# Incidence product of a graph network as one fp32r matmul of 258 columns, with a new order of the degree and edge steps

## The chip, the cores and the metric

One core of a Trainium2 chip runs the whole program. The metric is the time on the device in microseconds, from start to end of one execution. The kernel before took 1463.44 us in the median of three runs (1463.33 to 1463.59).

## The reference, cut to what matters

128 graphs with 128 nodes of 256 features go through four layers. Each layer's output is added to its input and normalised over the features. The first layer is a hypergraph convolution, used twice with one and the same operator; this change concerns its making:

```python
H  = (adj != 0).astype(x.dtype)                # incidence, 128 x 128
w  = adj.reshape(N, -1)[:, :C]                 # first row of adj
Dn = 1.0 / einsum('nce,ne->nc', H, w)          # where the sum is > 0
Be = 1.0 / H.sum(axis=1)                       # one value per hyperedge
G  = Dn * H @ (Be * H^T)                       # the operator of both convolutions
h  = layer_norm(relu(G (x W1^T) + b1), gamma, beta)
y  = G (h W2^T) + b2 + x
x  = _layernorm(x + y)
```

The second layer is a mean over the neighbours with two weights, the third has three graph convolutions, the fourth one graph convolution with a mask. Each is followed by the sum and `_layernorm`. The G line is the kernel's way of grouping, not a line of the reference.

## The kernel before, in words

The graphs are worked on in 64 pairs. The kernel is a software pipeline written out by hand: a table LAG says how many iterations after its start a pair reaches each stage, so that iteration n works on pair n in the stage G, on pair n-1 in R and P, on n-2 in xT, XAB and AXB, on n-3 in Ax2, H1, H1W and H2, on n-4 in H2W, AP3, Ax3 and TK, and on n-5 in the last normalisation F. Iterations 0 to 2 are written out in a function fill on each engine, iterations 3 to 68 run through a function body. Each engine has its own list of operations in a fixed order, and semaphores join them. Nothing is reordered: an operation that waits holds all that stands behind it on its engine.

TensorE (PE) works in the order R, G, xT, H2W, Ax2, XAB, H1, AP3, P, Tr, AXB, H1W, Ax3, Gx, GP, H2, TK (lines 499 to 533). Most products split both factors into a high part rounded to fp32r and a low part, the rest, and add three fp32r products (line 256). G, Tr, Gx, GP, xT, Ax2, Ax3 and H2 are plain fp32 instead.

The stages around the change, for pair q = n+1 (edges) and pair n (degrees):

- DVE makes the incidence HT (line 888), counts it (892), takes the maximum with 1 (897) and the reciprocal be_inv (904).
- POOL multiplies HT with be_inv into BH (1207). ACT copies the first row of the adjacency into BH's last column (weight_column, 645).
- In the next iteration PE forms G, per graph one fp32 product of HT with the 129 columns of BH into one bank (288). Column 128 of the result is the degree.
- DVE takes maximum (866), reciprocal (870) and the inverse degree dinv (874), and scales G's PSUM result into Gd (881). PE transposes Gd (303), ACT copies it out as GT (611).

In the body of the iteration DVE alternates degree and edge steps (lines 1085 to 1100). After them it makes the third normalisation's sum (1108), which waits for AP3, statistics, the split of XAB (858), the third's inverse and shift (828, 832), the variance of the hidden layer (921, 924), the reciprocal h_rstd (930), the operand p_f of GP (940), the aggregate (959), the second sum (969) and the first sum (976). ACT applies the third normalisation (560), takes the mean's square (623) and the root h_std (627). POOL's order is n_s (1246), the low parts r_lo (1188), two sums of squares (1194, 1196), A_lo, the fourth sum (1254), h_lo, BH (1207), x2c (1265), xb (1215), and h_lo of the second hidden layer.

## Time and profile before

| | |
|---|---|
| median of three runs | 1463.44 us |
| the profiled execution's own time | 1463.48 us |
| its span, first to last instruction | 1461.7 us |
| mean granted TensorE clock | 0.991 of full speed |
| busy: DVE, ACT, POOL | 1080.4, 1056.8, 851.7 us |
| data moved by DMA | 47.04 MB, mean 32 GB/s |

In the profile PE is TensorE's matmuls, PEld its weight loads, DVE VectorE, ACT ScalarE, POOL GpSimd. A matmul's end is modelled and overlaps the next one's start, so the distance between starts tells what one costs. An fp32 matmul appears as two records. A row of a timeline gives the start in us from the span's start, the duration of the row, the engine, the line, the operation, the tiles (output <- inputs), the shape and the number of instructions merged into the row; behind it stands the idle time of the engine before it, with what ended it. Line 254 is the helper that issues every matmul, line 541 ACT's copy, line 810 the statistics.

### The profile page before, as it was taken

Reading aid. Unit: us, or ns where it says so; the run is one execution under the profiler, and the core shown is the slowest. Engines: PE = TensorE matmul, PEld = TensorE weight load, DVE = VectorE, ACT = ScalarE, POOL = GpSimd, SP = SyncE. Lnnn points to the kernel's source line nnn. Section 1 sums busy time; section 2 is a strip of 40 time slices with the busy share of each in tenths; the row PEclk is TensorE's granted clock in tenths of the full one; section 3 lists DMA queues with packets and bytes.
Section 4 is the critical chain, followed back from the end, with each engine's and each line's share of the span. In section 5 each row is a group of like instructions: output and inputs, shape, how many; then the busy total and the mean of one; then the engine's idle time right before and its main releaser. Section 6 shows DMA issues by size and latency. Waiting matters only on the chain. (4 is left out here: it accounts for less than half of the span.)

```text
span 1461.7 us, 33281 instructions
## 1 busy us (share of the span) xinstructions
PE 1416.2 (97%) x10896; PEld 1353.8 (93%) x10896; DVE 1080.4 (74%) x3744; ACT 1056.8 (72%) x2442; POOL 851.7 (58%) x776
## 2 busy tenths in 40 slices
PE   7899999999999999999999999999999999999974
PEld 6799999999999999999999999999999999999973
DVE  6667777777777777777777777777777777777663
ACT  4577777778777777777777777777777777777863
POOL 4565565565566566566566566566566566566542
PEclk9999999999999999999999999999999999999997
DMA  4001101101101101101101101101100100110000
GB/s 135 23 12 37 38 19 37 38 19 37 37 20 37 38 19 37 38 19 37 38 20 37 38 19 37 38 24 32 38 26 30 38 28 29 37 30 16 15 16 22
DMA packets 29946, 47.04 MB, mean 32 GB/s; under 512 B 3408, under 2 KB 12240, under 8 KB 29776
## 3 DMA queue, kind: packets, MB, share of 16 engines
q1 hardware_dynamic: 29776, 44.91, 9.8%
q8 instruction: 89, 1.46, 0.4%
q14 instruction: 81, 0.66, 0.2%
HBM read 28.12 MB, written 16.78 MB: 31 GB/s over the span
## 5 line engine op out<-in xcount | busy, mean ns | idle before, releaser
L1180 POOL TENSOR_TENSOR h_lo<-h_f,h_hi 128x512 fp32r<-128x512 f32 x128 | 166.2, 1298 | 373.4 <-ACT h_hi L541 373.4
L560 ACT ACTIVATE x<-n_s,n_shift,n_rstd 128x256 f32<-128x256 f32 x384 | 208.4, 590 | 101.0 <-DVE n_shift L832 101.0
L810 DVE BATCH_NORM_STATS2 n_st<-n_s 128x6 f32<-128x256 f32 x512 | 188.1, 409 | 7.6 <-POOL n_s L1254 5.2
L555 ACT ACTIVATE n_std<-n_mv,eps_c 128x2 f32<-128x2 f32 x256 | 74.7, 292 | 158.3 <-DVE n_mv L815 158.2
L1188 POOL TENSOR_TENSOR r_lo<-r_f,r_hi 128x512 fp32r<-128x512 f32 x128 | 163.5, 1299 | 36.6 <-ACT r_hi L541 36.4
L1246 POOL TENSOR_TENSOR n_s<-tk,mask 128x512 f32<-128x512 f32 x64 | 66.7, 1042 | 165.7 <-issue 150.4
L254 PE MATMUL psum<-v_hi,h_hi 128*128 128x256 f32 x512 | 148.9, 291 | 5.0 <-issue 5.0
L254 PE MATMUL psum<-A_f,x 128*128 128x128 f32 x1024 | 142.1, 282 | 5.4 <-ACT x L560 4.8
L254 PE MATMUL psum<-w2c_hi,r_hi 128*128 128x258 f32 x512 | 145.9, 285 | 0.5 <-POOL r_lo L1188 0.5
L254 PE MATMUL psum<-w2c_hi,r_lo 128*128 128x258 f32 x512 | 146.0, 285 | 0.0
L254 PE MATMUL psum<-w2c_lo,r_hi 128*128 128x258 f32 x512 | 144.8, 283 | 0.0
L254 PE MATMUL psum<-v_hi,h_lo 128*128 128x256 f32 x512 | 144.1, 282 | 0.0
L254 PE MATMUL psum<-v_lo,h_hi 128*128 128x256 f32 x512 | 144.0, 281 | 0.0
L254 PE MATMUL psum<-gx_hi,w1T_hi 128*128 128x256 f32 x512 | 143.9, 281 | 0.0
L254 PE MATMUL psum<-gx_hi,w1T_lo 128*128 128x256 f32 x512 | 143.3, 280 | 0.0
L254 PE MATMUL psum<-gx_lo,w1T_hi 128*128 128x256 f32 x512 | 143.3, 280 | 0.0
L565 ACT ACTIVATE h_f<-psum,columns 128x256 f32<-128x256 f32 x256 | 107.7, 473 | 48.9 <-PE psum L254 48.9
L254 PEld LDWEIGHTS psum<-A_f,x 128*128 128x128 f32 x1024 | 126.0, 193 | 8.1 <-ACT x L560 5.4
L1108 DVE TENSOR_TENSOR n_s<-psum,x2c 128x512 f32<-128x512 f32 x64 | 44.3, 692 | 87.0 <-PE psum L254 87.0
L254 PE MATMUL psum<-wab_hi,x1T_hi 128*128 128x512 f32 x256 | 106.8, 417 | 0.0
L802 DVE TENSOR_TENSOR ax_lo<-psum,ax_hi 128x512 fp32r<-128x512 f32 x128 | 87.8, 686 | 25.3 <-ACT ax_hi L541 25.3
L565 ACT ACTIVATE r_f<-psum,columns 128x256 f32<-128x256 f32 x256 | 99.1, 463 | 3.9 <-PE psum L254 3.9
(141 smaller groups left out, 5044.1 us busy)
## 6 DMA issues: line engine op xcount, KB each, us to landing
x_in<-x_in_dram SPq DMA_DIRECT2D x64, 256.0 KB, 3.0
out<-x SPq DMA_DIRECT2D x64, 256.0 KB, 2.0
at_in<-adjT SPq DMA_DIRECT2D x64, 128.0 KB, 2.3
x<-v_in SPq DMA_DIRECT2D x3, 256.0 KB, 5.8
n_s<-w2T_in SPq DMA_DIRECT2D x2, 256.0 KB, 3.7
r_f<-w1T_in SPq DMA_DIRECT2D x2, 256.0 KB, 4.7
h_f<-wab_in SPq DMA_DIRECT2D x2, 256.0 KB, 6.0
rows<-rows_in SPq DMA_DIRECT2D x1, 256.0 KB, 6.1
```

The source lines that it names most:

```text
L254: return pe.matmul(o, a, b, start=start, stop=stop)
L555: act.activation(nm.std[:], nm.mv[:, :, 1], ACT.Sqrt, bias=eps_c[:, 0:1]).then_inc(nm.rooted, 1)
L560: last = act.activation(dst[:, g, :], nm.s[:, g, :], ACT.Identity, scale=nm.rstd[:, g:g + 1], bias=nm.shift[:, g:g + 1])
L565: return act.activation(dst[:, m].rearrange("p g c -> p (g c)"), psum[:, BANK[stage] + extra, (m % 2) * 2 * C:(m % 2 + 1) * 2 * C], ACT.Re ...
L802: return dve.tensor_tensor(dst[1][:], src, f(dst[0][:]), ALU.subtract).then_inc(signal, 1)
L810: last = dve.bn_stats(nm.st[:, g, :], nm.s[:, g, :])
L1108: dve.tensor_tensor(n3.s[:].rearrange("p g d -> p (g d)"), flat(BANK["AP3"]), x2c[(k - 4) % 2][:].rearrange("p g d -> p (g d)"), ALU.add). ...
L1180: return pool.tensor_tensor(dst[1][:], src, f(dst[0][:]), ALU.subtract).then_inc(signal, 1)
L1188: pool.tensor_tensor(r_s[1][:, half], r_f[:, half], f(r_s[0][:, half]), ALU.subtract).then_inc(r_lo[h], 1)
L1246: pool.tensor_tensor(n4.s[:], tk[:], bc(mask[:], [C, 2, D], 2), ALU.mult).then_inc(tk_masked, 1)
```

## The change

BH becomes 258 columns wide and fp32r: 128 columns of HT times the rounded be_inv (be_r), 128 of HT times the rest (be_rest), one with the rounded weight and one with its rest. HT is fp32r; it holds zeros and ones. One fp32r matmul per graph multiplies HT with all 258 columns, each graph into a bank of its own (5 and 7; for pair 2 6 and 7). ACT's weight_column becomes round_edges, which also rounds be_inv and stands behind out_XAB instead of ahead of it. POOL makes the two rests and two products. DVE first adds the two degree columns, then takes maximum, reciprocal and dinv from SBUF, scales the second half into Gl and adds the scaled first half, graph by graph. In the body the degree chain stands whole ahead of the four edge steps. ACT takes the hidden layer's mean square ahead of applying the third normalisation and h_std right behind it. DVE makes p and the aggregate ahead of the fourth normalisation's inverse and shift, and the second sum ahead of the split of Ax3. POOL's x2c waits for hve. Some banks and waits of the filling stage move.

```diff
-        HT = sb("HT", [2, C])
+        HT = sb("HT", [2, C], F32R)
-        BH = sb("BH", [2, C + 1])
+        BH = sb("BH", [2, 2 * C + 2], F32R)
...
             def G(n, k):
                 p = n
                 pe.wait_ge(bh_made, upto(p))
-                pe.wait_ge(w_made, upto(p))
+                pe.wait_ge(w_lo, upto(p))
+                if begun(p - 2) and not first(n, 2):
+                    pe.wait_ge(p_made, upto(p - 2))
                 if begun(p - 5):
                     pe.wait_ge(ax3_lo, upto(p - 5))
                 for g in range(2):
-                    last = mm(psum[:, BANK["G"], g * (C + 1):(g + 1) * (C + 1)], HT[:, g, :], BH[:, g, :],
-                              True, True)
+                    last = mm(psum[:, bank("G", p)[g], 0:2 * C + 2], HT[:, g, :], BH[:, g, :], True, True)
...
             def P(n, k):
...
+                if not first(n, 2):
+                    pe.wait_ge(gd_made, upto(n))
...
-            def weight_column(n, k):
+            def round_edges(n, k):
                 q = n + 1
                 act.wait_ge(at_loaded[(k + 1) % RING], at_count(q, k + 1))
                 if begun(n):
                     act.wait_ge(pe_did["G"], upto(n))
-                copy(BH[:, :, C:C + 1], at_in[:, (k + 1) % RING, :, 0:1]).then_inc(w_made, 1)
+                copy(BH[:, :, 2 * C:2 * C + 1], at_in[:, (k + 1) % RING, :, 0:1]).then_inc(w_hi, 1)
+                act.wait_ge(be_made, upto(q))
+                if begun(q - 1):
+                    act.wait_ge(bh_made, upto(q - 1))
+                copy(be_r[:], be_inv[:]).then_inc(be_hi, 1)
...
-                if active("prep", n):
-                    weight_column(n, k)
                 if active("XAB", n):
                     out_XAB(n, k)
+                if active("prep", n):
+                    round_edges(n, k)
...
                     root(n3, p)
+                if active("P", n):
+                    square_mean(n, k)
+                if active("AP3", n):
+                    p = n - 4
...
                     apply(n3, p, x3)
+                if active("P", n):
+                    root_h(n, k)
+                if active("Tr", n):
+                    copy_GT(n, k)
                 if active("F", n):
                     root(n4, n - 5)
-                if active("P", n):
-                    square_mean(n, k)
-                if active("Tr", n):
-                    copy_GT(n, k)
-                if active("P", n):
-                    root_h(n, k)
...
             def degree_max(n, k):
                 dve.wait_ge(pe_did["G"], upto(n))
-                dve.tensor_scalar(dn_max[:], dn, TINY, None, ALU.max).then_inc(dn_1, 1)
+                dve.tensor_reduce(dn[:], out_G(n, 2 * C, 2 * C + 2), AX_X, ALU.add).then_inc(dn_0, 1)
+                dve.wait_ge(dn_0, upto(n))
+                dve.tensor_scalar(dn_max[:], dn[:], TINY, None, ALU.max).then_inc(dn_1, 1)
...
-                dve.tensor_tensor(Gd[:], g_dn[:, :, 0:C], bc(dinv[:], [C, 2, C], 2), ALU.mult).then_inc(gd_made, 1)
+                dve.tensor_tensor(Gl[:], out_G(n, C, 2 * C), bc(dinv[:], [C, 2, C], 2), ALU.mult).then_inc(gl_made, 1)
+                dve.wait_ge(gl_made, upto(n))
+                for g in range(2):
+                    last = dve.scalar_tensor_tensor(out=Gd[:, g, :], in0=psum[:, bank("G", n)[g], 0:C],
+                                                    scalar=dinv[:, g:g + 1], in1=Gl[:, g, :],
+                                                    op0=ALU.mult, op1=ALU.add)
+                last.then_inc(gd_made, 1)
...
                 if active("G", n):
-                    degree_max(n, k)
+                    scale_G(n, k)
                 if active("prep", n):
-                    edges(n, k)
-                if active("G", n):
-                    degree_recip(n, k)
-                if active("prep", n):
-                    edge_count(n, k)
-                if active("G", n):
-                    degree_inverse(n, k)
-                if active("prep", n):
-                    edge_max(n, k)
-                if active("G", n):
-                    make_Gd(n, k)
-                if active("prep", n):
-                    edge_inverse(n, k)
+                    prep(n, k)
...
                 if active("AXB", n):
                     node_degree_max(n, k)
+                if active("AXB", n):
+                    node_degree_recip(n, k)
+                if active("P", n):
+                    wide_invert(n, k)
+                    make_p(n, k)
+                if active("AXB", n):
+                    make_agg(n, k)
                 if active("F", n):
                     invert(n4, n - 5)
-                if active("P", n):
-                    wide_invert(n, k)
+                    shift(n4, n - 5)
                 if active("AXB", n):
-                    node_degree_recip(n, k)
-                if active("F", n):
-                    shift(n4, n - 5)
-                if active("P", n):
-                    make_p(n, k)
-
-                if active("AXB", n):
-                    make_agg(n, k)
+                    sum_n2(n, k)
                 if active("Ax3", n):
                     dve.wait_ge(ax3_hi, upto(n - 4))
                     split_lo(ax3, flat(BANK["Ax3"]), ax3_lo)
-                if active("AXB", n):
-                    sum_n2(n, k)
...
             def make_BH(n, k):
                 q = n + 1
-                pool.wait_ge(be_made, upto(q))
+                pool.wait_ge(w_hi, upto(q))
+                pool.tensor_tensor(BH[:, :, 2 * C + 1:2 * C + 2], at_in[:, (k + 1) % RING, :, 0:1],
+                                   f(BH[:, :, 2 * C:2 * C + 1]), ALU.subtract).then_inc(w_lo, 1)
+                pool.wait_ge(be_hi, upto(q))
+                pool.tensor_tensor(be_rest[:], be_inv[:], f(be_r[:]), ALU.subtract).then_inc(be_lo, 1)
                 if begun(n):
                     pool.wait_ge(pe_did["G"], upto(n))
-                pool.tensor_tensor(BH[:, :, 0:C], HT[:], bc(be_inv[:], [C, 2, C], 2), ALU.mult).then_inc(bh_made, 1)
+                pool.tensor_tensor(BH[:, :, 0:C], f(HT[:]), bc(f(be_r[:]), [C, 2, C], 2), ALU.mult)
+                pool.wait_ge(be_lo, upto(q))
+                pool.tensor_tensor(BH[:, :, C:2 * C], f(HT[:]), bc(be_rest[:], [C, 2, C], 2),
+                                   ALU.mult).then_inc(bh_made, 1)
...
                     pool.wait_ge(n2.done, upto(p))
+                    if active("P", n):
+                        pool.wait_ge(hve, upto(n - 1))
```

## Rows read from the trace of the kernel before

**Rows 1.** The page, part 1: busy time, share of the span and instructions.
```profile
PE 1416.2 (97%) x10896; PEld 1353.8 (93%) x10896; DVE 1080.4 (74%) x3744; ACT 1056.8 (72%) x2442; POOL 851.7 (58%) x776
```
**Rows 2.** Timeline of PE in one iteration in the middle.
```profile
814.98 0.61 PE L254 MATMUL psum<-BH,HT 128*128 128x129 f32 x4
815.43 0.65 PE L368 MATMUL psum<-ident,x 128*128 128x128 f32 x4
...
822.45 0.28 PE L254 MATMUL psum<-h2w_hi,A_hi 128*128 128x256 f32 x1
...
823.16 0.28 PE L254 MATMUL psum<-w2c_hi,r_hi 128*128 128x258 f32 x1
...
828.81 1.14 PE L254 MATMUL psum<-A_f,x 128*128 128x128 f32 x8
829.79 1.06 PE L254 MATMUL psum<-GT,x_in 128*128 128x128 f32 x8
```
**Rows 3.** Timeline of ACT, same iteration.
```profile
814.03 0.29 ACT L555 ACTIVATE n_std<-n_mv,eps_c 128x2 f32<-128x2 f32 x1 [0.20 <-DVE n_mv L815]
...
818.64 0.62 ACT L541 ACTIVATE ax_hi<-psum 128x512 fp32r<-128x512 f32 x1
...
822.65 0.84 ACT L565 ACTIVATE h_f<-psum,columns 128x256 f32<-128x256 f32 x2 [0.34 <-PE psum L254]
...
827.65 1.09 ACT L560 ACTIVATE x<-n_s,n_shift,n_rstd 128x256 f32<-128x256 f32 x2 [1.60 <-DVE n_shift L832]
...
829.40 0.20 ACT L627 ACTIVATE h_std<-h_veps 128x2 f32<-128x2 f32 x1
...
835.85 0.29 ACT L555 ACTIVATE n_std<-n_mv,eps_c 128x2 f32<-128x2 f32 x1 [0.20 <-DVE n_mv L815]
```
**Rows 4.** Timeline of DVE, same iteration.
```profile
819.90 0.15 DVE L866 TENSOR_SCALAR dn_max<-psum 128x2 f32<-128x2 f32 x1
...
821.63 0.41 DVE L881 TENSOR_TENSOR Gd<-psum,dinv 128x256 f32<-128x256 f32 x1
...
823.36 0.69 DVE L1108 TENSOR_TENSOR n_s<-psum,x2c 128x512 f32<-128x512 f32 x1 [1.25 <-PE psum L254]
...
826.56 0.97 DVE L832 SCALAR_TENSOR_TENSOR n_shift<-n_mv,n_rstd 128x2 f32<-128x2 f32 x1
...
829.84 0.88 DVE L940 SCALAR_TENSOR_TENSOR p_f<-psum,h_rstd,betaW 128x256 f32<-128x256 f32 x2
...
832.01 0.68 DVE L969 SCALAR_TENSOR_TENSOR n_s<-agg,x 128x512 f32<-128x512 f32 x1
...
833.22 0.67 DVE L976 SCALAR_TENSOR_TENSOR n_s<-xb,psum 128x512 f32<-128x512 f32 x1
```
**Rows 5.** Groups of DVE by line and shape, 600 to 1000 us: busy, mean ns.
```profile
L897 DVE TENSOR_SCALAR be<-ht_count 128x2 f32<-128x2 f32 x19 | 13.1, 688 | 0.0
...
L892 DVE TENSOR_REDUCE ht_count<-HT 128x2 f32<-128x256 f32 x19 | 8.0, 421 | 0.0
```
**Rows 6.** Timeline of DVE in the filling stage, POOL idle.
```profile
3.70 0.17 DVE L897 TENSOR_SCALAR be<-ht_count 128x2 f32<-128x2 f32 x1
```
**Rows 7.** Timeline of POOL, the iteration of rows 2 to 4.
```profile
817.84 2.54 POOL L1188 TENSOR_TENSOR r_lo<-r_f,r_hi 128x512 fp32r<-128x512 f32 x2 [0.42 <-ACT r_hi L541]
820.34 1.35 POOL L1194 TENSOR_TENSOR sq<-sq 128x512 f32<-128x512 f32 x1
...
822.46 0.74 POOL L1180 TENSOR_TENSOR A_lo<-at_in,A_hi 128x256 fp32r<-128x256 f32 x1
823.15 1.30 POOL L1254 TENSOR_TENSOR n_s<-n_s,x 128x512 f32<-128x512 f32 x1
824.40 1.30 POOL L1180 TENSOR_TENSOR h_lo<-h_f,h_hi 128x512 fp32r<-128x512 f32 x1
825.64 0.63 POOL L1207 TENSOR_TENSOR BH<-HT,be_inv 128x256 f32<-128x256 f32 x1
...
827.46 1.30 POOL L1215 TENSOR_TENSOR xb<-x_in,b2half 128x512 f32<-128x512 f32 x1
```

More of the change, by code:

```diff
@@ L25 @@
 BANK = dict(R=0, Ax2=0, Tr=0, GP=0, H1=1, Gx=1, XAB=2, AXB=2, TK=2, H2=3, xT=4, P=4,
-            H2W=6, H1W=6, G=7, AP3=7, Ax3=7)
+            H2W=6, H1W=6, G=(5, 7), AP3=7, Ax3=7)
 BANKS = 8
@@ L67, in build @@
         at_in = sb("at_in", [RING, 2, C])
-        HT = sb("HT", [2, C])
-        ht_count, be, be_inv = sb("ht_count", [2]), sb("be", [2]), sb("be_inv", [2])
-        BH = sb("BH", [2, C + 1])
-        dn_max, dn_inv, dinv = sb("dn_max", [2]), sb("dn_inv", [2]), sb("dinv", [2])
-        Gd = sb("Gd", [2, C])
+        HT = sb("HT", [2, C], F32R)
+        ht_count, be = sb("ht_count", [2]), sb("be", [2])
+        be_inv, be_r, be_rest = sb("be_inv", [2]), sb("be_r", [2], F32R), sb("be_rest", [2])
+        BH = sb("BH", [2, 2 * C + 2], F32R)
+        dn, dn_max, dn_inv, dinv = sb("dn", [2]), sb("dn_max", [2]), sb("dn_inv", [2]), sb("dinv", [2])
+        Gl, Gd = sb("Gl", [2, C]), sb("Gd", [2, C])
         GT = [sb(f"GT{b}", [2, C]) for b in range(2)]
@@ L132, in build @@
         pe_R0 = sem("pe_R0")
-        ht_made, ht_counted, be_max, be_made, bh_made = (
-            sem(s) for s in ("ht_made", "ht_counted", "be_max", "be_made", "bh_made"))
-        dn_1, dn_2, dn_3, gd_made = sem("dn_1"), sem("dn_2"), sem("dn_3"), sem("gd_made")
-        w_made, gt_made, gx_hi, gx_lo = (sem(s) for s in ("w_made", "gt_made", "gx_hi", "gx_lo"))
+        ht_made, ht_counted, be_max, be_made, be_hi, be_lo, bh_made = (
+            sem(s) for s in ("ht_made", "ht_counted", "be_max", "be_made", "be_hi", "be_lo", "bh_made"))
+        dn_0, dn_1, dn_2, dn_3, gl_made, gd_made = (sem(s) for s in ("dn_0", "dn_1", "dn_2", "dn_3", "gl_made", "gd_made"))
+        w_hi, w_lo, gt_made, gx_hi, gx_lo = (sem(s) for s in ("w_hi", "w_lo", "gt_made", "gx_hi", "gx_lo"))
         r_relu, r_hi = [sem(f"r_relu{j}") for j in range(2)], [sem(f"r_hi{j}") for j in range(2)]
@@ L170, in bank @@
         def bank(stage, pair):
+            if stage == "G" and pair == 2:
+                return 6, 7
             if stage == "Tr" and pair in (1, 2):
-                return 3
+                return 3 * pair
             if stage == "GP" and pair == 0:
@@ L296, in Tr @@
                     pe.wait_ge(eye_loaded, 16)
-                if first(n, 2):
-                    pe.wait_ge(betaW_made, 1)
                 pe.wait_ge(gd_made, upto(p))
@@ L363, in xT @@
                 pe.wait_ge(n1.done, upto(p))
-                if not first(n, 2):
+                if first(n, 2):
+                    pe.wait_ge(betaW_made, 1)
+                else:
                     pe.wait_ge(p_made, upto(p))
@@ L655, in fill @@
                 act.wait_ge(table_loaded, 1)
-                weight_column(-1, -1)
+                round_edges(-1, -1)
                 act.wait_ge(columns_loaded, 16)
@@ L661, in fill @@
                 split_w1(1)
-                weight_column(0, 0)
+                round_edges(0, 0)
                 relu_r(1, 1, 0)
@@ L677, in fill @@
                 root_h(1, 1)
+                round_edges(1, 1)
                 relu_r(2, 2, 0)
@@ L695, in fill @@
                 out_XAB(2, 2)
+                round_edges(2, 2)
                 for dst, src in ((v_s[2], v_f[2]), (wk_s, wk_f)):
@@ L859, in split_xbw, with out_G @@
                                   f(xbw[0][:, :, 0:D]), ALU.subtract).then_inc(xbw_lo, 1)
-            g_dn = psum[:, BANK["G"], 0:2 * (C + 1)].rearrange("p (g c) -> p g c", g=2)
-            dn = g_dn[:, :, C]
+            def out_G(n, lo, hi):
+                b = bank("G", n)
+                return psum[:, b[0]:b[1] + 1:b[1] - b[0], lo:hi]
             def degree_max(n, k):
                 dve.wait_ge(pe_did["G"], upto(n))
-                dve.tensor_scalar(dn_max[:], dn, TINY, None, ALU.max).then_inc(dn_1, 1)
+                dve.tensor_reduce(dn[:], out_G(n, 2 * C, 2 * C + 2), AX_X, ALU.add).then_inc(dn_0, 1)
+                dve.wait_ge(dn_0, upto(n))
+                dve.tensor_scalar(dn_max[:], dn[:], TINY, None, ALU.max).then_inc(dn_1, 1)
             def degree_recip(n, k):
@@ L873, in degree_inverse @@
                 dve.wait_ge(dn_2, upto(n))
-                dve.scalar_tensor_tensor(out=dinv[:], in0=dn, scalar=0.0, in1=dn_inv[:],
+                dve.scalar_tensor_tensor(out=dinv[:], in0=dn[:], scalar=0.0, in1=dn_inv[:],
                                          op0=ALU.is_gt, op1=ALU.mult).then_inc(dn_3, 1)
@@ L1009, in fill @@
                 split_gx(0, 0)
+                prep(0, 0)
                 split_w1(1)
@@ L1148, in body @@
                     make_agg(n, k)
+                if active("F", n):
+                    invert(n4, n - 5)
+                    shift(n4, n - 5)
+                if active("AXB", n):
+                    sum_n2(n, k)
                 if active("Ax3", n):
```

12 lines of the change are left out of this document (3 added, 9 removed).

## The prediction

> **What bounds the kernel now.** I read the page first, then the timeline of each engine over one iteration in the middle (pair p enters at iteration n = p), because the average says little here: PE is busy for 97% of the span [rows 1]. In the PE timeline the reader is to see that stages follow each other without a hole, and also that the modelled busy time hides small waits: eight passes of 128 columns run in 0.98 us at the Ax3 stage (828.81 to 829.79), although a pass of that width takes 0.11 us (G's four passes fill 814.98 to 815.43), which makes 0.89 [rows 2]. So the Ax3 stage waits 0.09 us, for the third normalisation.
>
> In the DVE and ACT timelines I look for a chain that closes on itself. ACT's root of the first normalisation starts at 814.03 and the next at 835.85, 21.82 us later [rows 3]. From the first, ACT works on without a gap to the copy ax_hi at 818.64; DVE takes over (ax_lo, degree chain, third sum at 823.36), ACT normalises (827.65) and takes the root h_std (829.40), DVE makes p (829.84), the sums at 832.01 and 833.22, and the statistics that release 835.85 [rows 3, 4]. In this chain DVE waits for PE only once, for the third sum at 823.36, after Gd was done at 822.04 (821.63 + 0.41). The kernel is therefore held by two things of nearly one length: PE's work, and this chain through DVE and ACT. A saving on PE is worth its price only if the chain shortens too.
>
> A third view, DVE's groups, shows what the chain is sensitive to. The two-element maximum be takes 0.69 us in the loop and 0.17 us in the filling stage when POOL is idle [rows 5, 6]. In the loop it ends when POOL's sum of squares ends (820.34 + 1.35 = 821.69). In the same way the shift at 826.56 takes 0.97 us and ends at 827.53, where POOL's x2c hands over to xb (827.46) [rows 4, 7]. DVE operations that read and write SBUF alone can thus be held until the running POOL operation ends; Gd, which reads PSUM, starts beside POOL at 821.63 and takes its 0.41 us.
>
> **PE's part.** Removed: four passes of G, 0.45 us. Added: two fp32r matmuls of 258 columns. The row nearest to them is the third product, six fp32r matmuls of 256 columns in 0.71 us (822.45 to 823.16), 0.118 us each [rows 2]; I take 0.12, so 0.24 us. PE saves 0.21 us in each iteration. Bounds: 0.17 (a switch of format costing 0.02 a matmul) to 0.23. The Trainium skill, "TensorE: Matmul & The Clock Gate", section "Back-to-back issue gap", gives N/2.4 + 2.5 ns, an estimate of 0.110 us for 258 columns; by it PE would save 0.23 us. The trace's 0.118 decides. The waits of PE on p_made (for the bank) and of P on gd_made cost nothing: p is a whole iteration old at G, and the third product ahead of P waits for gd_made already.
>
> **The degree chain (DVE).** I walk the new order in the clock of this iteration, with ax_hi at 818.64 as fixed point, since ACT's run from 814.03 to there is unchanged. A dependent two-element step costs 0.17 [rows 6] and some 0.03 to hand over.
> - The reduction of the two degree columns reads PSUM and takes the place of dn_max: 819.90 to 820.06.
> - dn_max now reads SBUF. It asks at 820.10; POOL's r_lo runs until 820.38 (817.84 + 2.54) [rows 7]. Done 820.41. The reciprocal ends at 820.61.
> - dinv now reads two SBUF tiles, as the held shift does. It asks at 820.65, and POOL's sum of squares has been running since 820.34. Done about 821.74.
> - Gl, like Gd before, 0.41: 821.78 to 822.19. Two halves of 128 columns, by the 0.41 of Gd less half its columns at about one nanosecond each, 0.30 each: Gd is done at 822.8, against 822.04 before. The third product is due at 822.45, so PE waits 0.4 us there.
> Bounds for Gd: 821.7 if neither step is held, 823.0. I take 822.8, because both held forms have a row.
>
> **The edges behind it.** HT asks at 822.74 while POOL makes A_lo (until 823.20): done 823.35. The count takes 0.42 [rows 5], to 823.8. The maximum be then asks while POOL makes the fourth sum (from about 823.2, 1.30 long) and is held until 824.5, as it was held before until 821.69. be_inv is done at 824.7, and the third sum starts at 824.65 instead of 823.36: 1.3 us late [rows 4, 7].
>
> **ACT.** round_edges waits for be_made at 824.7. Queued behind it are the relus h_f (822.65 before) and their rounding. The two-element copy takes about 0.20, like h_std; h_f starts at 824.85, and 0.84 + 0.62 (the length of ax_hi) later h_hi is done at 826.4 [rows 3]. POOL's h_lo moves from 824.40 to 826.4 and ends at 827.7, 2.0 us later; its user on PE, H1W, is itself pushed back by the 0.4 of the third product and stands behind the whole of P, so I take nothing for it and keep 0.2 as the upper bound.
>
> **POOL.** After h_lo come two small subtractions and two products instead of one. The small ones have no row: POOL's 256 elements take 0.74 and 512 take 1.30 [rows 7], which leaves 0.18 of fixed cost; bounds 0.1 and 0.3. The products take 0.63 each. So BH is ready at about 829.2, x2c (behind its new wait for hve, which is earlier) runs until 830.45, and xb until 831.7, against 828.76 before. For the next G this is hidden, there being some 7 us to it; for the lock it is not.
>
> **Third normalisation and what follows.** From third sum to shift is 3.20 us (823.36 to 826.56): it asks at 827.85, between POOL operations, and is done at 828.0 instead of 827.53. This is where the old hold of 0.83 goes. The normalisation takes 1.09 from 828.1, h_std 0.20 behind it, so p starts at 829.55, 0.3 us earlier than 829.84: placing the mean square ahead and the DVE reciprocals in time takes the old detour away. p and agg take 1.57 together (832.01 less 0.60 for ax_lo less 829.84), to 831.12. Now the inverse and the shift of the fourth normalisation stand here: the shift asks at 831.3 and is held by xb until 831.73. The second sum starts at 831.77, ax_lo 0.60 later, gx_lo, and the first sum at 833.57 instead of 833.22. **The chain is 0.35 us longer**, 22.17 instead of 21.82.
>
> **Sum.** 59 iterations hold all stages (n = 5 to 63): 59 x 0.35 = 20.7 us. The filling stage gets ACT's copy, POOL's subtraction and second product, and the longer scaling ahead of the first graph products: 0.2 + 0.2 + 0.6 + 0.8, less what the shorter G gives; I take 2 us, bounds 0 and 5. The profiled execution took 1463.48 us (span 1461.7), as good as the median of 1463.44. Forecast 1463.5 + 20.7 + 2 = 1486.
>
> The Trainium skill speaks against the change at just this point: "SBUF — State Buffer", section "SBUF: two separate sides", says that a DVE operation with two SBUF inputs or in a 2-port mode and a GpSimd operation exclude each other for a whole instruction. The trace agrees for be and the shift; by that rule the new dn_max and dinv join them.
>
> **The rivals.**
> - *The chain keeps its length.* If xb is done by 831.3 (small POOL operations shorter, h_lo earlier), the shift of the fourth is free and the first sum starts at 833.15: nothing gained, nothing lost in the loop. 1463.5 + 2 = 1465.5, and with a few hundredths either way 1461 to 1470. For it: only 0.4 us separates the two. Against it: between h_lo and xb POOL has no idle time in which to catch up.
> - *Faster, PE decides.* If the two-element steps are not held, or be slips in between two POOL operations, the third sum starts as soon as PE delivers it. Then the 0.21 of G and the 0.09 ahead of Ax3 count, and as much again ahead of the product with p, which the earlier p removes: 59 x 0.4 = 24 us, 1442 with the filling stage. With only dinv held, PE's 0.4 us wait before the third product takes that back and 59 x 0.08 = 5 us less 2, about 1461, is left. The point from which it decides is a third sum before about 824.1. For it: p_f, agg and the sums would all have slack. Against it: be is held in the mean of 19 rows.
> - *Slower still.* The shift of the third meets the first product of POOL (0.63) instead of a gap: 0.3 to 0.5 us more an iteration, 1504 to 1515.
> - *The product isn't faster.* If fp32r with 258 columns ran in two passes, PE would keep its 0.45 us; with the chain as the bound the forecast would stand.
>
> **How the numbers follow.** The chain longer with xb in the way 0.48; the chain unchanged 0.20; PE decides, wholly or in part, 0.25; slower still 0.07. About 0.2% (3 us) is what a measurement of this kernel can tell from no change. Of the unchanged case I give 0.12 to within 3 us, 0.06 to slower and 0.02 to faster, and 0.01 of the PE case lies within too; so faster 0.26, same 0.13, slower 0.61. The range runs from 1450, which leaves out the full PE case (0.12), to 1498, which leaves out the last (0.07). The forecast case's own range is 1474 to 1498.
>
> **What would show it.** BH,HT as two matmuls 0.12 apart; dinv at about 1.1 us instead of 0.15; be still at 0.5 to 0.7; the third sum no longer waiting for PE; ACT's h_f waiting for be_inv; n_shift short at the third and long at the fourth; PE with idle time ahead of the transposes of x1 and the third product. A third sum that still waits for PE would prove me wrong, whatever the total.

## The result, and the profile after

The changed kernel takes 1473.88 us (median of 4 runs, 1473.70 to 1474.56) against 1463.51 us beside it: a ratio of 1.007, 95% interval 1.0052 to 1.0087. That is slower by 10.4 us, a little less than half of the 22.5 us forecast. Spans of the profiled executions: 1471.9 us after, 1461.7 us before.

The page, part 1 (answers to [rows 1]):
```profile
PE 1408.7 (96%) x10768; PEld 1350.3 (92%) x10768; DVE 1213.3 (82%) x3936; ACT 1061.1 (72%) x2506; POOL 907.9 (62%) x968
```
DVE is busy for 133 us more. dinv alone is about 55 of them (0.15 us before, 1.01 now, 64 times): two elements for each row, which wait for POOL. "Held" below means this, a DVE operation whose row is long because a POOL operation is running.

The times below are of one iteration in which ax_hi starts at 825.76. It started at 818.64 in the iteration of [rows 3], so **take off 7.12 us to compare a time with the forecast or with rows of before**.

Timeline of PE (answers to [rows 2]):
```profile
822.45 0.41 PE L257 MATMUL psum<-BH,HT 128*128 128x258 f32 x2
822.69 0.60 PE L374 MATMUL psum<-ident,x 128*128 128x128 f32 x4
...
829.52 0.28 PE L257 MATMUL psum<-ax_hi,v_lo 128*128 128x256 f32 x1
830.03 0.36 PE L257 MATMUL psum<-h2w_hi,A_hi 128*128 128x256 f32 x1 [0.23 <-DVE Gd L898]
...
836.43 1.08 PE L257 MATMUL psum<-A_f,x 128*128 128x128 f32 x8
837.35 1.06 PE L257 MATMUL psum<-GT,x_in 128*128 128x128 f32 x8
```
G fills 0.24 us (822.45 to 822.69) instead of 0.45. The third product now waits for Gd: at 0.12 us for a matmul it would start at 829.64, and it starts 0.39 us later. The distance from Ax3 to Gx is 0.92 us, against 0.98.

Timeline of ACT (answers to [rows 3]):
```profile
821.15 0.29 ACT L560 ACTIVATE n_std<-n_mv,eps_c 128x2 f32<-128x2 f32 x1 [0.20 <-DVE n_mv L826]
...
825.76 0.62 ACT L546 ACTIVATE ax_hi<-psum 128x512 fp32r<-128x512 f32 x1
...
831.82 0.20 ACT L546 ACTIVATE be_r<-be_inv 128x2 fp32r<-128x2 f32 x1 [2.22 <-DVE be_inv L924]
831.93 0.82 ACT L570 ACTIVATE h_f<-psum,columns 128x256 f32<-128x256 f32 x2
...
835.20 1.10 ACT L565 ACTIVATE x<-n_s,n_shift,n_rstd 128x256 f32<-128x256 f32 x2 [0.73 <-DVE n_shift L843]
836.20 0.19 ACT L632 ACTIVATE h_std<-h_veps 128x2 f32<-128x2 f32 x1
...
843.06 0.30 ACT L560 ACTIVATE n_std<-n_mv,eps_c 128x2 f32<-128x2 f32 x1 [0.20 <-DVE n_mv L826]
```
One root of the first normalisation follows the other after 21.91 us, against 21.82 in [rows 3]. Over all full iterations the means are 21.917 and 21.841 us (distance of PE's stage R from one pair to the next). This distance is called the period below.

Timeline of DVE (answers to [rows 4]):
```profile
827.21 0.33 DVE L880 TENSOR_SCALAR dn_max<-dn 128x2 f32<-128x2 f32 x1
...
827.77 1.01 DVE L888 SCALAR_TENSOR_TENSOR dinv<-dn,dn_inv 128x2 f32<-128x2 f32 x1
828.82 0.42 DVE L895 TENSOR_TENSOR Gl<-psum,dinv 128x256 f32<-128x256 f32 x1
829.27 0.61 DVE L898 SCALAR_TENSOR_TENSOR Gd<-psum,dinv,Gl 128x128 f32<-128x128 f32 x2
829.80 0.61 DVE L908 TENSOR_SCALAR HT<-at_in 128x256 fp32r<-128x256 f32 x1
...
830.90 0.69 DVE L917 TENSOR_SCALAR be<-ht_count 128x2 f32<-128x2 f32 x1
831.62 0.17 DVE L924 RECIPROCAL be_inv<-be 128x2 f32<-128x2 f32 x1
831.73 0.69 DVE L1116 TENSOR_TENSOR n_s<-psum,x2c 128x512 f32<-128x512 f32 x1
...
834.93 0.16 DVE L843 SCALAR_TENSOR_TENSOR n_shift<-n_mv,n_rstd 128x2 f32<-128x2 f32 x1
...
835.19 0.47 DVE L944 SCALAR_TENSOR_TENSOR h_veps<-h_var,eps_c 128x2 f32<-128x2 f32 x1
...
836.62 0.88 DVE L960 SCALAR_TENSOR_TENSOR p_f<-psum,h_rstd,betaW 128x256 f32<-128x256 f32 x2
837.42 0.87 DVE L979 SCALAR_TENSOR_TENSOR agg<-psum,rdeg,xa 128x256 f32<-128x256 f32 x2
...
838.39 0.31 DVE L843 SCALAR_TENSOR_TENSOR n_shift<-n_mv,n_rstd 128x2 f32<-128x2 f32 x1
838.62 0.68 DVE L989 SCALAR_TENSOR_TENSOR n_s<-agg,x 128x512 f32<-128x512 f32 x1
...
840.42 0.68 DVE L996 SCALAR_TENSOR_TENSOR n_s<-xb,psum 128x512 f32<-128x512 f32 x1
```
dinv takes 1.01 us. The third sum follows be_inv without a gap and no longer waits for PE.

Timeline of POOL (answers to [rows 7]):
```profile
827.47 1.29 POOL L1199 TENSOR_TENSOR sq<-sq 128x512 f32<-128x512 f32 x1
828.84 0.73 POOL L1201 TENSOR_TENSOR sq<-sq 128x256 f32<-128x256 f32 x1
...
830.21 1.35 POOL L1266 TENSOR_TENSOR n_s<-n_s,x 128x512 f32<-128x512 f32 x1
833.49 1.28 POOL L1185 TENSOR_TENSOR h_lo<-h_f,h_hi 128x512 fp32r<-128x512 f32 x1 [1.93 <-ACT h_hi L546]
834.73 0.20 POOL L1210 TENSOR_TENSOR BH<-at_in,BH 128x2 fp32r<-128x2 f32 x1
...
835.03 0.61 POOL L1216 TENSOR_TENSOR BH<-HT,be_r 128x256 fp32r<-128x256 f32 x1
835.60 0.61 POOL L1218 TENSOR_TENSOR BH<-HT,be_rest 128x256 fp32r<-128x256 f32 x1
836.17 1.28 POOL L1279 TENSOR_TENSOR x2c<-x,rows 128x512 f32<-128x512 f32 x1
837.41 1.27 POOL L1227 TENSOR_TENSOR xb<-x_in,b2half 128x512 f32<-128x512 f32 x1
```
dinv ends at 828.78, with the sum of squares (827.47 + 1.29 = 828.76). be ends at 831.59, with the fourth sum (831.56). The second sum starts at 838.62, as xb ends (838.68).

**Where the 10.4 us are.** Three marks in each trace divide the difference of the two spans, 10.2 us: G of pair 5 (the end of the filling stage), the period, and the rest.

| | before | after | difference |
|---|---|---|---|
| G of pair 5 starts | 94.53 | 99.14 | +4.6 |
| 59 periods | 59 x 21.841 | 59 x 21.917 | +4.5 |
| the rest, to the end of the span | 78.6 | 79.7 | +1.1 |

### The profile page after: what moved, and what is told of

It reads as the page before. It is cut to its first block and busy times, and to the rows that moved or that the text cites. A ratio compares the mean times of both kernels' runs of the same rounds, so it can differ in the third digit from the quotient of the medians.

```text
span 1471.9 us, 33596 instructions
## 1 busy us (share of the span) xinstructions
PE 1408.7 (96%) x10768; PEld 1350.3 (92%) x10768; DVE 1213.3 (82%) x3936; ACT 1061.1 (72%) x2506; POOL 907.9 (62%) x968
## 5 line engine op out<-in xcount | busy, mean ns | idle before, releaser
L546 ACT ACTIVATE be_r<-be_inv 128x2 fp32r<-128x2 f32 x64 | 13.0, 203 | 133.6 <-DVE be_inv L924 133.6
L257 PEld LDWEIGHTS psum<-v_hi,h_hi 128*128 128x128 f32 x512 | 97.3, 190 | 5.5 <-issue 5.5
```

Of the source, the lines that this page charges most:

```text
L257: return pe.matmul(o, a, b, start=start, stop=stop)
L546: return act.activation(o, i, ACT.Copy)
```

## The experiments

Each ran beside the kernel before (medians 1463.2 to 1464.4 us). The period is the mean over some 55 iterations.

### Degree sums in PSUM

```diff
+        dn = psum[:, 7, 510:512]
-        dn, dn_max, dn_inv, dinv = sb("dn", [2]), ...
+        dn_max, dn_inv, dinv = ...
```


> The changed kernel, but the sum of the two degree columns is left in PSUM, so that the maximum and dinv read PSUM. Theory 1 (the chain through DVE, ACT and POOL is the bound, and dinv is held by POOL's sum of squares): dinv 0.15 us instead of 1.01, Gd 1.1 to 1.2 us earlier, the third sum waits for PE again, period 21.4 us instead of 21.91, so 1474 - 59 x 0.5 = 1444 us. Rival A (PE's own work grew: it reads the wider fp32r operand, its first stage R takes 2.86 instead of 2.82 us): the period stays within 0.1 us of 21.9, 1468 to 1474. Rival B (ACT's wait for be_made is what costs, not the degrees): be_made comes only about 0.6 to 1 us earlier and ACT still waits; the gain is about half, 1455 to 1465.

Measured: 1436.78 us, ratio 0.9807 (0.9789 to 0.9826), period 21.322. That is theory 1, with 37 us instead of its 30; both rivals are out. Timeline of DVE:
```profile
806.37 0.16 DVE L881 TENSOR_SCALAR dn_max<-psum 128x2 f32<-128x2 f32 x1
...
806.76 0.16 DVE L889 SCALAR_TENSOR_TENSOR dinv<-psum,dn_inv 128x2 f32<-128x2 f32 x1
...
807.94 0.28 DVE L909 TENSOR_SCALAR HT<-at_in 128x256 fp32r<-128x256 f32 x1
...
808.72 0.17 DVE L918 TENSOR_SCALAR be<-ht_count 128x2 f32<-128x2 f32 x1
...
809.63 0.69 DVE L1117 TENSOR_TENSOR n_s<-psum,x2c 128x512 f32<-128x512 f32 x1 [0.54 <-PE psum L258]
```
and of POOL:
```profile
806.61 1.31 POOL L1200 TENSOR_TENSOR sq<-sq 128x512 f32<-128x512 f32 x1
808.00 0.82 POOL L1202 TENSOR_TENSOR sq<-sq 128x256 f32<-128x256 f32 x1
```
dinv runs in the middle of the sum of squares. be, now earlier, comes 0.1 us before POOL's short sum ends (808.82) and is hardly held. The third sum waits for PE again. So 37.1 us of the changed kernel's time (1473.9 less 1436.8) are this one placement of two numbers per row.

### All the new orders on the old product

```diff
@@ body of before, DVE, ACT and POOL @@
+   the degree chain whole, ahead of the four edge steps
+   ACT: square_mean ahead of apply(n3), root_h and copy_GT behind it
+   DVE: wide_invert, make_p, make_agg ahead of invert(n4), shift(n4)
+   POOL: wait_ge(hve, ...) ahead of x2c
```


> The kernel before with all the new orders (degrees ahead of edges, mean square ahead of the third normalisation, DVE's tail, x2c behind hve), but the old fp32 product with 129 columns and one product on POOL. Theory 1: no degree step reads SBUF beside POOL's sum of squares, so nothing there is held; the third shift is free, the waits of PE ahead of Ax3 and of the product with p go; period 21.84 - 0.28 = 21.56, 1447 us. Rival A: the orders are worth nothing by themselves, 1463. A third possibility, that x2c pushed back delays xb and with it the fourth shift: 1455 to 1463.

Measured: 1446.32 us, ratio 0.9873 (0.9856 to 0.9891), period 21.560, as theory 1 said. The orders alone gain 17 to 18 us; the wide product on top of them costs 27.6 us (1473.9 less 1446.3).

### The wide product in the old orders

```diff
@@ body of after @@
-   all four lines above
```


> The wide fp32r product with all that it needs, but degrees and edges alternating as before, ACT's and DVE's old orders, x2c without its wait. Theory 1: dn_max is held by r_lo, HT by the sum of squares, be by A_lo, all ahead of Gd in the alternating order; Gd comes about 1.5 us later than in the changed kernel, PE waits some 1.9 us ahead of the third product, period about 23.3 us, 1550 us. Rival A (PE's own work): as the changed kernel or less, 1463 to 1475. Rival B (ACT's wait): about as the changed kernel, 1470 to 1480.

Measured: 1501.92 us, ratio 1.0256 (1.0235 to 1.0276), period 22.378. The direction holds; the size is less than half of what was expected (38 us over the kernel before instead of 87). Timeline of DVE:
```profile
806.95 0.81 DVE L942 SCALAR_TENSOR_TENSOR h_veps<-h_var,eps_c 128x2 f32<-128x2 f32 x1
...
820.56 0.28 DVE L906 TENSOR_SCALAR HT<-at_in 128x256 fp32r<-128x256 f32 x1
...
821.21 0.80 DVE L886 SCALAR_TENSOR_TENSOR dinv<-dn,dn_inv 128x2 f32<-128x2 f32 x1
821.93 0.16 DVE L915 TENSOR_SCALAR be<-ht_count 128x2 f32<-128x2 f32 x1
```
h_veps is held by xb (in POOL's timeline 806.46, 1.28 long). dinv is held until 822.01, and be, asked right behind it, is not held at all although POOL has its next sum to do. That sum starts at 822.07: it waits for the sum before it, and the two stand 0.08 us apart in every version here, so be passes in a pause of POOL's own.

### Degrees and edges alternating again, the rest as changed

```diff
-                    scale_G(n, k)
-                    prep(n, k)
+                    degree_max(n, k)
+                    edges(n, k)
+                    degree_recip(n, k)
...
```


> The changed kernel with degrees and edges alternating as before, all else new. Theory 1: as for the product alone, Gd 1.5 us later, 1540 to 1550 us. Rival B (ACT's wait for be_made): be_made comes at about the same time as in the changed kernel, so 1470 to 1478.

Measured: 1478.71 us, ratio 1.0098 (1.0076 to 1.0121), period 21.971. A miss of theory 1: I expected each two-element step to meet a POOL operation of its own. In the trace dn_max is released at POOL's boundary and HT, queued right behind it, goes through unheld in 0.28 us. Of the two-element steps of degrees and edges dn_max keeps its 0.33, only dinv is held for long (0.80 us), and be takes 0.15. Two chains interleaved share a boundary. Rival B's number was nearly met (1470 to 1478), but not for its reason: be_inv comes earlier than in the changed kernel, and the third sum waits for PE again. A hold has moved elsewhere as well, to the shift of the second normalisation, which meets POOL's h_lo (it takes 0.15 us in the changed kernel). Timeline of DVE:
```profile
811.77 0.69 DVE L1128 TENSOR_TENSOR n_s<-psum,x2c 128x512 f32<-128x512 f32 x1 [1.06 <-PE psum L257]
...
822.93 0.89 DVE L843 SCALAR_TENSOR_TENSOR n_shift<-n_mv,n_rstd 128x2 f32<-128x2 f32 x1
```
That hold isn't what sets the period, since the version with the sums in PSUM has it too (0.89 us) at 21.32. Gd does: it ends 4.25 us after ax_hi's start instead of 4.12, the third product starts 0.15 us behind it in both, and 0.13 us more than the 21.84 of the version without the maximum (below) is 21.97.

### The wide product in the old orders, sums in PSUM

The edits of the wide product in the old orders and of the PSUM version together.

> The wide product with the orders of the kernel before, and the two degree sums kept in PSUM. Theory (two separate costs: SBUF-only two-element steps held behind POOL, and an order in which the mean square stands behind the third normalisation): only the hold of dinv goes (0.80 us in the wide product with the old orders), h_veps stays held by POOL's xb (0.81 us there), so the period falls from 22.38 by 0.1 to 0.3 us, to 22.1 to 22.3, 1484 to 1496 us. Rival (the degree chain alone was the price of the wide product): the period falls to that of the kernel before less what G saves, 21.6 to 21.7, 1450 to 1456 us.

Measured: 1489.19 us, ratio 1.0179 (1.0162 to 1.0196), period 22.207, in the middle of the theory's range. dinv takes 0.15, h_veps still 0.82, be 0.69. The PSUM sums are worth 12.7 us in the old orders and 37.1 in the new ones.

### The maximum with 1 left out

```diff
-                dve.tensor_scalar(be[:], ht_count[:], 1.0, None, ALU.max)...
-                dve.reciprocal(be_inv[:], be[:]).then_inc(be_made, 1)
+                dve.reciprocal(be_inv[:], ht_count[:]).then_inc(be_made, 1)
```


> The changed kernel without the maximum of the edge count with 1 (left out; every edge here has members, and the inverse is taken of the count itself). The held two-element step is gone, so be_inv and the third sum can come 0.5 to 0.7 us earlier. Theory (one chain through the third sum sets 21.92, but a second loop through Gd, the third product, R, the relus and ax_hi stands 0.07 us behind it at about 21.84): the period falls only to 21.84 to 21.86, 1469 to 1471 us, with the wait of the third product for Gd unchanged at about 0.4 us. Rival A (one chain only): the period falls by 0.5 us or so to 21.4, 1440 to 1447 us. Rival B (be's hold passes on to be_inv, which now meets the same POOL operation): unchanged, 1473 to 1475 us.

Measured: 1467.98 us, ratio 1.0029 (1.0012 to 1.0045), period 21.839. The gain stops at the second loop, as the theory said (21.84), and the third product still waits 0.41 us for Gd. A saving of 0.7 us on the chain gave 0.078.

### The fourth normalisation's steps back ahead of p

```diff
                     node_degree_max(n, k)
+                    invert(n4, n - 5)
                     wide_invert(n, k)
                     node_degree_recip(n, k)
+                    shift(n4, n - 5)
                     make_p(n, k)
...
```


> The changed kernel with DVE's operations behind the third normalisation in the order of the kernel before (inverse and shift of the fourth ahead of p and of the node degree's inverse, ax3_lo ahead of the second sum). Theory of the second loop: the shift of the fourth, asked earlier, falls between or into POOL's products and p is late by what it is held; if it isn't held the first chain shortens by up to 0.17 us and the loop through Gd caps the gain at 21.84, 1469 us. Rival: the order of the tail is worth what the forecast's last steps say, the shift held 0.3 to 0.5 us ahead of p, which is on the chain: period 22.2 to 22.4, 1490 to 1502 us.

Measured: 1493.49 us, ratio 1.0206 (1.0190 to 1.0221), period 22.259. p starts 1.18 us after h_std instead of 0.42 (836.62 less 836.20). DVE waits there for ACT's root of the fourth, and the shift is held 0.38 us. The rival of the expectation was right.

### ACT's old order in the changed kernel

```diff
                     root(n3, p)
-                    square_mean(n, k)
                     apply(n3, p, x3)
-                    root_h(n, k)
-                    copy_GT(n, k)
                     root(n4, n - 5)
+                    square_mean(n, k)
+                    copy_GT(n, k)
+                    root_h(n, k)
...
-                        pool.wait_ge(hve, upto(n - 1))
```


> The changed kernel with ACT's order of before (mean square, copy of GT and root of h behind the application of the third normalisation and the root of the fourth), without POOL's wait for hve. Theory (the order is worth about as much here as on the old product, 0.2 to 0.5 us an iteration, since h_veps is then asked behind the hand-over to xb and is held by it): period 22.2 to 22.4, 1490 to 1502 us. Rival (after the third sum's own lateness of 1.2 us the mean square has slack): period 21.92 to 21.98, 1474 to 1478 us.

Measured: 1543.73 us, ratio 1.0549 (1.0532 to 1.0565), period 23.090. The theory's direction, three times its size. Where DVE waits in the middle of the kernel (for what, us in total, times, longest):
```profile
DVE h_var L939 <- ACT h_mean L628: 78.9, 53, 1.8
```
ACT comes to the mean only behind the application of the third normalisation, which is itself late, and the root of the fourth. DVE idles 1.5 us for it in each iteration (78.9 by 53), and h_veps behind it is held for 0.70. Beside a degree chain that stands in front, the move of the mean square is worth 1.17 us an iteration; beside alternating chains it was 0.41, with p's move (22.378 less 21.971).

### Each order alone on the old product

```diff
@@ body of before: square order only @@
+   ACT, DVE (p, agg) and POOL lines of the new orders
@@ body of before: degree order only @@
+   the degree chain whole, ahead of the four edge steps
```


> The kernel before with two of the change's orders: ACT's mean square, root of h and copy of GT ahead of the third normalisation's application and of the fourth's root, and DVE's p and agg ahead of the fourth's inverse and shift (with POOL's wait for hve). Old product, degrees and edges still alternating. Theory (the whole gain of 17 to 18 us that all orders together give on the old product comes from here, since in before the third sum waits for PE and Gd is in time anyhow): period 21.55 to 21.60, 1446 to 1449 us. Rival (the two reorderings need each other): less than half of it, 1455 to 1463 us.

> The kernel before with the degree chain ahead of the edges on DVE and nothing else. Theory (Gd comes about 1 us earlier, but nobody waits for it; the third sum is held by PE): no change, 1462 to 1465 us. Rival (the edges behind it end later, be meets POOL's next operation, and the third sum waits for be_inv instead of for PE): 0.1 to 0.4 us an iteration more, 1469 to 1487 us.

Measured: 1445.47 us, ratio 0.9878 (0.9863 to 0.9893), period 21.560; and 1460.24 us, ratio 0.9980 (0.9970 to 0.9989), period 21.770. The whole gain of the orders is the mean square ahead and p ahead, with POOL's wait for hve; these were not separated on the old product. The degree chain ahead of the edges brings 3 us alone (I expected none) and nothing beside the other.

### ACT's copies earlier in the filling stage (fill_only, psum_fill)

```diff
+                round_edges(1, 1)
                 square_mean(1, 1)
                 root_h(1, 1)
-                round_edges(1, 1)
...
+                round_edges(2, 2)
                 out_XAB(2, 2)
-                round_edges(2, 2)
```
First in the changed kernel:

> The changed kernel with ACT's two-element copies in the filling stage put earlier: those for graph 2 ahead of the first mean square and root, those for graph 3 ahead of the copies of the products with x_a. Theory (of the 4.6 us that the filling stage costs more than before, about half is BH of the second graph coming at 31.9 us instead of 25.3, which pushes xb and then holds wab_lo, 2.78 instead of 1.28 us): the product G of pair 5 comes 1.5 to 3 us earlier than at 99.14 us, the period stays 21.92, total 1471 to 1472.5 us. Rival (the filling stage pays for the longer scaling of the first graphs, two steps held by POOL): less than 0.5 us, 1473.5 to 1474 us.

Measured: 1476.77 us (1473.24 to 1479.39), ratio 1.0090 (1.0070 to 1.0109), period 21.929, G of pair 5 at 103.20 us instead of 99.14. A miss: the filling stage got longer, although what the edit aimed at happened (xb at 30.78 us instead of 33.29, wab_lo 1.28 us instead of 2.78). The profiled execution is the slowest of the four (1479.39); in the medians the loss is 2.9 us.

Then in the version with the sums in PSUM:

> The version with the degree sums in PSUM (1436.8 us), with ACT's two-element copies of the filling stage put earlier as in fill_only. There the earlier copies brought the first edges and xb forward but the filling stage got 2 to 3 us longer, with TensorE's granted clock at 0.56 to 0.76 in 40 to 50 us where it had been 0.94 to 1.00. Theory (the filling stage is ruled by where TensorE pauses long enough for its clock to fall, so an earlier copy on ACT is as likely to cost as to gain; nothing of the loop changes): period 21.32, product G of pair 5 between 96 and 101 us against 97.84, total 1434.5 to 1440 us. Rival (fill_only lost its time through POOL's hold of the two-element steps, which is absent here): G of pair 5 at 95 to 96 us, 1433.5 to 1435 us.

Measured: 1433.94 us, ratio 0.9799 (0.9782 to 0.9816), period 21.322, G of pair 5 at 94.77 us instead of 97.84. The same edit that cost 4.1 us there brings 3.1 here (2.8 in the medians), and this is the fastest version. The rival's total was met (1433.5 to 1435) and the theory's was not, but the rival's reason isn't shown, since the granted clock differs as well. The view of windows from 45 to 50 us, first of the slower filling stage (fill_only), then of this one. Behind the length of the stretch stand the busy us and instructions of PE, PEld, DVE, ACT and POOL, then the granted clock as a share of full speed, the DMA share and GB/s:
```profile
45.00:50.00 5.00, 5.00 (x15) 3.94 (x15) 1.85 (x6) 1.94 (x5) 1.53 (x4) 0.56 0.12 44
```
```profile
45.00:50.00 5.00, 4.05 (x32) 3.87 (x32) 4.71 (x13) 0.64 (x2) 4.58 (x4) 1.00 0.00 0
```
At 0.56 the granted clock is near the lower of its two levels, 1.2 of 2.4 GHz: PE is busy throughout and starts 15 matmuls in 5 us. The changed kernel has 1.00 in this stretch and its low stretches elsewhere (0.52 in 20 to 25 us, 0.72 in 35 to 40). What moves them was not tested; dn_max of pair 2 is held as long in the slower one (1.25 us) as in the changed kernel (1.26). Over the first 94 us the mean granted clock (the view of windows) goes roughly with the time of G of pair 5:

| | before | changed | fill_only | sums in PSUM | psum_fill |
|---|---|---|---|---|---|
| granted clock | 0.95 | 0.93 | 0.89 | 0.93 | 0.96 |
| G of pair 5, us | 94.53 | 99.14 | 103.20 | 97.84 | 94.77 |

From the changed kernel to fill_only the shortfall from full clock grows by 0.04 x 94 = 3.8 us, and G comes 4.1 later; between the two versions with the sums in PSUM it shrinks by 0.03 x 94 = 2.8 us, and G comes 3.1 earlier. By this estimate, an upper bound since PE isn't busy all of that time, the clock can account for most of what the edit did both times, but only for 1.9 of the 4.6 us between the kernel before and the changed one.

### The fourth shift behind the second sum (shift4_late)

```diff
-                    invert(n4, n - 5)
-                    shift(n4, n - 5)
                     sum_n2(n, k)
+                    invert(n4, n - 5)
+                    shift(n4, n - 5)
```


> The changed kernel with the fourth normalisation's inverse and shift behind the second sum on DVE instead of ahead of it. Theory (the second sum stands 0.35 us later than p and agg would let it, for the inverse and the shift, which ends with POOL's xb; that is in the chain that sets 21.92, and the loop through Gd caps at 21.84): period 21.84 to 21.86, 1469 to 1471 us. Rival A (the fourth shift isn't in the chain): 21.92, 1473 to 1475 us. Rival B (the shift behind the second sum is late for the fourth normalisation on ACT and so for the relus of the next graph): 22.0 to 22.3, 1478 to 1497 us.

Measured: 1494.17 us, ratio 1.0210 (1.0185 to 1.0235), period 22.260. The chain did not shorten, since the second sum reads agg and x, both in SBUF, and is held by xb itself:
```profile
829.36 0.91 DVE L989 SCALAR_TENSOR_TENSOR n_s<-agg,x 128x512 f32<-128x512 f32 x1
...
830.38 0.16 DVE L843 SCALAR_TENSOR_TENSOR n_shift<-n_mv,n_rstd 128x2 f32<-128x2 f32 x1
```
The inverse and the shift, which used to pass in xb's shadow, now stand behind its end. The first sum comes 0.2 us later, and the fourth normalisation, later too, moves POOL's h_lo onto the second's shift (0.32 us). Rival B was right, near the top of its range: ACT waits 0.56 us for that shift ahead of the fourth normalisation and the relus behind it.

### One more small operation on POOL (be_rest_twice)

```diff
+                pool.tensor_tensor(be_pad[:], be_inv[:], f(be_r[:]), ALU.subtract)
                 pool.tensor_tensor(be_rest[:], be_inv[:], f(be_r[:]), ALU.subtract).then_inc(be_lo, 1)
```


> The changed kernel with POOL's two-element subtraction be_rest done twice (the first into a tile that nobody reads), so that the products of BH, x2c and xb all end 0.15 us later and nothing else on the path changes. Theory (p and agg are ready, the fourth shift ends with xb and the second sum starts with its end, so xb's end sets the chain): the fourth shift 0.46 instead of 0.31 us, period 21.917 + 0.15 = 22.07, 59 x 0.15 = 9 us, 1482 to 1484 us; the forecast had xb end 0.14 us later than it did, so this is the size of its error there. Rival (xb's end has slack to the chain, and the loop's lateness comes by be and the third sum alone): period 21.92 to 21.95, 1473.5 to 1476 us.

Measured: 1484.40 us, ratio 1.0138 (1.0119 to 1.0157), period 22.078, as the theory said (22.07). Timeline of POOL, then of DVE:
```profile
844.92 1.27 POOL L1229 TENSOR_TENSOR xb<-x_in,b2half 128x512 f32<-128x512 f32 x1
```
```profile
845.67 0.53 DVE L844 SCALAR_TENSOR_TENSOR n_shift<-n_mv,n_rstd 128x2 f32<-128x2 f32 x1
846.12 0.68 DVE L990 SCALAR_TENSOR_TENSOR n_s<-agg,x 128x512 f32<-128x512 f32 x1
```
An operation of 0.15 us on an engine busy for 62% of the span costs 10.5 us: 0.16 us in each of 59 iterations are 9.5, and the rest lies outside the loop. The shift is held until xb ends (846.19), and the second sum starts with that end. So in the changed kernel a later end of xb lengthens every iteration by as much. An earlier one was not tested alone; the shift takes 0.31 us there against 0.16 free, so at most about 0.15 us could be won at this point.

## Why the prediction was right in its steps and wrong in its size

**PE's part: right.** 0.24 us for G, and 0.4 us of waiting ahead of the third product (0.39 in the trace). The two fp32r matmuls stand 0.12 us apart. One sign did not come: the transposes of x1 start right behind G (822.69), without idle time ahead of them.

**The degree chain: right to 0.1 us.** Less 7.12, dinv ends at 821.66 (forecast 821.74) and Gd at 822.76 (822.8). Moving the sums to PSUM removed the hold and 37 us, which shows the cause. The trace agrees with the rule of the Trainium skill ("SBUF — State Buffer", "SBUF: two separate sides"), that a DVE operation with two SBUF inputs and a GpSimd operation exclude each other, in the 1.01 us of dinv; with one input in PSUM it took 0.16.

**The edges and the third sum: right.** be at 0.69, the third sum at 824.61 (forecast 824.65), behind be_inv instead of PE. What I had not seen is a second loop close behind, through Gd and the third product, 21.84 us long, on which the version without the maximum stopped. It bears on a rival too: with only dinv held the forecast left a gain of 0.08 us, while its own terms, 0.4 won and 0.4 waited, leave nothing. The version without the maximum comes near that case, and its period, 21.839, is that of the kernel before, 21.841.

**Third normalisation: right.** The shift is free (0.16), p starts at 829.50 (829.55). One hold I had overlooked, h_veps at 0.47 us, is over 0.5 us before ACT is ready for h_std and costs nothing.

**Where it failed: the last step, "the second sum starts at 831.77".** This is the end of the sum that makes the chain 0.35 us longer. The second sum started at 831.50, and everything behind it came 0.27 us earlier: the first sum at 833.30 instead of 833.57. About half is the end of xb, forecast at 831.7 and measured at 831.56, the sum of small errors in POOL's row of operations. The rest is the hand-over: I let the second sum start 0.04 us after the shift's end, and it started 0.08 before it, as DVE's records in a row overlap here. Against 833.22 before, that leaves +0.08 us where I had +0.35. be_rest_twice shows that the step decides: it moved the end of xb by 0.15 and the period by 0.16. The term was therefore 4.5 us and not 20.7. I had priced this point in a rival ("if xb is done by 831.3"), and the truth lay between the two cases, at 831.56. What I took for two cases was one scale. That the loop came out longer at all is in part luck: it rests on 0.08 us out of steps that were forecast to within some 0.1, and more than half of the 10.4 us lies outside the loop.

**The filling stage: 4.6 us instead of 2.** I had counted the work added, 1.8 us. The trace shows two things that I left out: dinv held for 1.16 us in G of pair 1 and dn_max for 1.26 in that of pair 2; and ACT's copies for the second graph standing behind root_h, so that xb came at 33.29 instead of 25.86 and met wab_lo (2.78 instead of 1.28 us). Their shares stay open, since fill_only, made to separate them, changed the granted clock as well; the changed kernel's own lower clock (0.93 against 0.95 over the first 94 us) is a third. The last 1.1 us behind the loop were not in the forecast and were not traced to a step; the granted clock of the last 80 us is 0.86, against 0.90 in the last 79 of the kernel before.

**The orders against the product.** The forecast treated the change as one sum. The runs split it (us, medians):

| | old product | wide, sums in SBUF | wide, sums in PSUM |
|---|---|---|---|
| old orders | 1463.5 | 1501.9 | 1489.2 |
| degree chain ahead | 1460.2 | 1543.7 (p ahead too) | not run |
| mean square and p ahead | 1445.5 | 1478.7 | not run |
| both | 1446.3 | 1473.9 | 1436.8 |

So the change holds a gain of 18 us from the order of ACT's and DVE's steps, a gain of 0.21 us of PE's time in each iteration, which pays only when DVE keeps up (1446.3 to 1436.8; in the spans 59 x 0.24 = 14.0 us in the loop, less 3.3 in the filling stage and 1.7 behind the loop), and a loss of 37 us from reading two sums in SBUF. At 21.322 us a period PE's stages follow each other without the waits of the changed kernel ahead of the third product. PE is then what the version in PSUM is held by, as far as the rows tell: there the third sum waits for PE, and Gd is ready 0.7 us before the third product.

## What to carry to other kernels

When a small operation is moved from PSUM to SBUF operands, look at what POOL runs at that moment: the two-element step costs the rest of POOL's operation, up to 1.0 us in the loop here, and keeping the intermediate in PSUM took that away. Where the forecast hinges on the end of one operation that holds the next, give the time as a slope (so much later end, so much longer period) and not as two cases, and test it by adding a small operation. Change an order and a data path in separate versions: one gained 18 us here and the other lost 28.

## What the hardware showed that I had not expected

- **A row of DVE operations goes through one boundary together.** In the alternating order HT behind a held dn_max took 0.28 us and be behind a held dinv 0.16, where they take 0.61 and 0.69 in the changed kernel. POOL pays: the sum of squares that met HT took 1.41 us instead of 1.29. The boundary behind dinv is a special one, as POOL pauses there for 0.08 us of its own. The Trainium skill ("SBUF — State Buffer", "SBUF: two separate sides") says that whichever operation starts first has the ports for its whole length. The trace agrees, and adds that at the boundary the waiting DVE operation, with HT behind it, went ahead of POOL's next one.
- **Taking a held operation away moves the hold.** With the fourth shift gone from in front of it, the second sum was itself held by xb (0.91 us instead of 0.68).
- **The filling stage has a time of its own.** The same edit of ACT's copies was worth +4.1 us in one version and -3.1 in the other (profiled executions), with the granted clock at 0.56 and 1.00 over the same 5 us and at 0.89 and 0.96 over the first 94.
